# Rows of B and C written twice, one product in four moved to GpSimd, squares moved before a seam's decays: an audio tower with a selective scan on one core

## The chip, the cores and the metric

The kernel runs on one core of a Trainium2 chip. The metric is the device time of one execution in microseconds. The engines work in parallel, each through its own list of instructions in order, and wait for one another by semaphores: TensorE (PE, with its weight loads PEld), VectorE (DVE), ScalarE (ACT), GpSimd (POOL), and SyncE (SP), which here issues every DMA.

## The reference

Inputs are 64 series of 750 samples, cut into 10 overlapping patches of 128, so 640 tokens of width 512. The core of the reference, shortened:

```
h = patches @ W.T + b                                  # tokens, width 512
hid = layernorm(h);  x = rmsnorm(hid)
z, xv, B, C, dt_in = split(x @ in_proj_w.T)            # 1024, 256, 256, 1024, 128
dt = softplus(dt_in @ dt_proj_w.T + dt_proj_b)         # 1024 channels
state[ch, n] = exp(dt * A[ch, n]) * state[ch, n] + dt * xg[ch] * B[ch, n]   # 16 states, over 10 steps
y[ch] = sum_n C[ch, n] * state[ch, n] + D_skip * xg[ch]
mid = hid + (y * silu(z)) @ out_proj_w.T
h = h + mid + swiglu(rmsnorm(mid))                     # width 2048
h = h + swiglu(layernorm(h))                           # width 2048
```

## The kernel before

Tokens lie in the free dimension, channels on the 128 partitions. The tokens are worked in two chunks, of 290 and of 350 tokens (29 and 35 series of 10 steps). The scan is cut into **units**: for each of 8 tiles m of 128 channels, four units q of four states each, so 32 units a chunk, numbered u = 0 to 31 and 32 to 63. A partition of a unit holds one channel and four states; the width of a unit is 4 x 290 or 4 x 350 elements.

One unit goes through five engines. SP loads its rows of B into `bb` (L367) and of C into `cb` (L383), each row repeated over partitions. They come from `b_rows` and `c_rows` in DRAM, where SP has stored the projections five times over (L402 and L371), so that every unit's rows lie together. POOL multiplies dt * x (`dtx`, L443) by B into `hs` (L453), the input of the recurrence. ACT makes the decays exp(dt * A) in `da` (L551), a PSUM ring of ND = 4 pieces. DVE scans, four pieces a unit (L781), in place in `da`, and multiplies two pieces at a time by C into `hs` (L792). In chunk 0 PE adds the four states with an identity matrix into the bank `SUM` (L1000), unit u - 2 in the middle of slot u, and unit 31 at the end of slot 32. In chunk 1 POOL does these sums (`add_states`, L466 to L482). When a tile's four units are summed, DVE adds the skip and gates by z (L807, L813).

`hs` has NH = 4 slots. The input of unit u (L453) waits until the unit that held its slot has been summed: `h_summed` in chunk 0 (PE), `added` in chunk 1 (POOL).

All else is written into the **slots** of `schedule()`, one a unit, and every engine's program is made from that list, some kinds of step with a lag (`late`). In chunk 0's slots stand the projections of its later tiles (`in_c`, `in_z`, `dtp` for dt, `xs` for x), then, from unit 14 on, the norms of chunk 1 (`tokc`, `mean`, `ln1`, `rms1`), its projections and its first tiles. In chunk 1's slots stand chunk 0's output projection (`out`), and its two MLPs (`gu`, `down`), each led by a norm (`rms2`; `ln2_mean` and `ln2_var`). After unit 63 come chunk 1's own output and MLPs, which PE alone sets. A **seam** in this text is one of the two places where chunk 1's last projections (the steps in `SEAM`) stand beside a norm of chunk 0: there ACT makes four squares (L586), PE adds them over channels, ACT takes the inverse root (L592, L593), and DVE scales (L864, L880), before PE can start an MLP.

On ACT a slot is: decays of the unit's pieces 2 and 3, a first part of the steps, decays of pieces 0 and 1 of the next unit, the second part. POOL's slot is: the input of unit u + 1, the sums of unit u - 1, softplus of a tile (L488 to L492). SP's is: `load_b(u + 3)`, `load_c(u + 2)`. PSUM banks of the projections form a ring of three, later four. ACT loads a function table (L528) when it changes between ln/exp, silu and tanh.

## Time and profile before

| | us |
|---|---|
| median of 3 runs (lowest, highest) | 679.44 (677.98, 681.44) |
| the profiled execution, its own time | 676.66 |
| its span | 674.7 |
| PE busy in the span | 630.5 |
| DVE, POOL, ACT busy | 425.5, 428.9, 329.3 |

The profile is one execution, with the time of each instruction and, for each wait, the instruction that ended it. Some 2 us lie outside its span. The granted clock is TensorE's clock as a share of full speed, 1.00 being 2.4 GHz and 0.50 being 1.2 GHz. A float32 matmul is recorded as two instructions, so x8 is four matmuls.

### The profile page before, as it was taken

The numbers are of one execution on the slowest core, as the hardware profiler recorded it, in microseconds if no ns is written. First come the engines' busy times: TensorE is split into PE (matmuls) and PEld (weight loads), VectorE is DVE, ScalarE is ACT, GpSimd is POOL, SyncE is SP. The second block draws the span as 40 slices with busy tenths as digits, with TensorE's granted clock in tenths as the row PEclk, the third lists the DMA queues.
The fourth block names the chain that finished last, engine by engine and source line by source line (L and its number), as shares of the span: only waits on it lengthen the run. The fifth ranks groups of instructions, "written<-read, shape, count | busy, mean of one in ns | idle before, by whom it ended". The sixth has DMA issues, their size and how long they took to land.

```text
span 674.7 us, 8618 instructions
## 1 busy us (share of the span) xinstructions
PE 630.5 (93%) x2846; PEld 505.2 (75%) x2846; DVE 425.5 (63%) x660; ACT 329.3 (49%) x646; POOL 428.9 (64%) x244
## 2 busy tenths in 40 slices
PE   4959998799999979999979999999999999999998
PEld 3637675466665657777747777766999998999998
DVE  4087997889987859889887988861322223332132
ACT  4358888458887363323346323321642443543441
POOL 0276786348787999887877988644455464445561
PEclk9979999799999979999989999999999999999999
DMA  8799997599999949989866998634443353144421
GB/s 339 253 358 365 316 312 245 169 280 371 336 375 373 362 176 359 412 334 332 316 247 231 345 326 317 200 124 113 140 153 127 124 157 125 63 128 131 147 67 43
DMA packets 49164, 163.50 MB, mean 242 GB/s; under 512 B 4320, under 2 KB 18528, under 8 KB 48480
## 3 DMA queue, kind: packets, MB, share of 16 engines
q1 hardware_dynamic: 49120, 162.95, 69.6%
q8 instruction: 23, 0.38, 0.2%
q14 instruction: 21, 0.17, 0.1%
HBM read 145.24 MB, written 17.69 MB: 242 GB/s over the span
## 4 chain that ended last, share of the span: by engine, by line
PE 73%; DVE 12%; ACT 4%; POOL 4%; issue 3%; DMA 2%; SPq 0%; DVEq 0%; ACTq 0%; POOLq 0%
PE work L990 53%; PE da L990 15%; DVE da L781 7%; PE work L1000 5%; DVE hs L792 3%; POOL hs L453 2%; ACT L528 1%; DMA bb<-b_rows 1%; ACT da L551 1%; DMA c_rows<-c_rows 1%; DMA sm<-small 1%; POOL acc L479 0%; POOL acc L477 0%; POOL hs L466 0%; DVE a L847 0%
## 5 line engine op out<-in xcount | busy, mean ns | idle before, releaser
L781 DVE TENSOR_TENSOR_SCAN da<-da,hs 128x290 f32<-128x290 f32 (+1 forms) x256 | 198.1, 817 | 35.1 <-POOL hs L453 21.2
L453 POOL TENSOR_TENSOR hs<-dtx,bb 128x1160 f32<-128x1160 f32 (+1 forms) x64 | 171.1, 2674 | 59.6 <-PE work L1000 52.4
L551 ACT ACTIVATE da<-dt,a_neg 128x261 f32<-128x261 f32 (+1 forms) x256 | 118.4, 495 | 144.7 <-DVE hs L792 144.5
L432 POOL TENSOR_TENSOR ws<-wraw,ws 128x1024 fp32r<-128x1024 f32 x40 | 101.5, 2538 | 92.8 <-ACT ws L559 92.8
L990 PE MATMUL work<-sq,wraw 128*128 128x290 f32 x512 | 126.0, 407 | 1.5 <-DVE sq L880 1.1
L990 PE MATMUL work<-hn,win 128*128 128x290 f32 (+1 forms) x336 | 103.6, 457 | 17.4 <-DVE hn L855 8.0
L990 PEld LDWEIGHTS work<-sq,wraw 128*128 128x128 f32 x512 | 96.5, 189 | 30.8 <-issue 1.8
L792 DVE TENSOR_TENSOR hs<-da,cb 128x580 f32<-128x580 f32 (+1 forms) x128 | 105.3, 822 | 10.2 <-DMA cb<-c_rows 3.5
L990 PEld LDWEIGHTS work<-hn,win 128*128 128x128 f32 x336 | 65.7, 200 | 51.3 <-issue 26.1
L559 ACT CAST ws<-wraw 128x1024 fp32r<-128x1024 f32 x48 | 50.3, 1048 | 70.6 <-PE da L990 34.4
L990 PE MATMUL work<-hn,ws 128*128 128x350 f32 x480 | 79.2, 323 | 1.6 <-DVE hn L951 1.6
L990 PEld LDWEIGHTS work<-hn,ws 128*128 128x128 f32 x480 | 77.3, 189 | 1.9 <-issue 1.9
L1000 PE MATMUL work<-hs,sm 128*128 128x290 f32 x256 | 67.8, 408 | 0.0
L990 PE MATMUL work<-gated_n,wraw 128*128 128x290 f32 x256 | 63.3, 407 | 0.0
L1000 PEld LDWEIGHTS work<-hs,sm 128*128 128x128 f32 x256 | 48.5, 190 | 16.3 <-DVE hs L792 0.5
L990 PEld LDWEIGHTS work<-gated_n,wraw 128*128 128x128 f32 x256 | 48.5, 189 | 14.2
L990 PE MATMUL da<-hn,ws 128*128 128x350 f32 x288 | 47.5, 323 | 0.0
L990 PE MATMUL da<-gated,ws 128*128 128x350 f32 x288 | 47.0, 323 | 0.0
L990 PEld LDWEIGHTS da<-gated,ws 128*128 128x128 f32 x288 | 46.5, 189 | 0.0
L990 PEld LDWEIGHTS da<-hn,ws 128*128 128x128 f32 x288 | 46.4, 189 | 0.0
L899 DVE TENSOR_TENSOR pair<-th,work 128x350 f32<-128x350 f32 x20 | 10.4, 520 | 56.7 <-PE work L990 50.6
L477 POOL TENSOR_TENSOR acc<-acc,hs 128x700 f32<-128x700 f32 x16 | 26.7, 1666 | 19.6 <-DVE hs L792 19.6
(97 smaller groups left out, 630.8 us busy)
## 6 DMA issues: line engine op xcount, KB each, us to landing
wraw<-w_stream SPq DMA_DIRECT2D x104, 512.0 KB, 3.8
bb<-b_rows SPq DMA_DIRECT2D x32, 700.0 KB, 6.7
cb<-c_rows SPq DMA_DIRECT2D x32, 700.0 KB, 5.5
bb<-b_rows SPq DMA_DIRECT2D x32, 580.0 KB, 8.2
cb<-c_rows SPq DMA_DIRECT2D x32, 580.0 KB, 6.2
c_rows<-c_rows SPq DMA_DIRECT2D x8, 875.0 KB, 11.0
c_rows<-c_rows SPq DMA_DIRECT2D x8, 725.0 KB, 6.4
win<-w_in SPq DMA_DIRECT2D x4, 1024.0 KB, 13.1
```

Of the source, the lines that this page charges most:

```text
L432: nc.gpsimd.tensor_tensor(ws[:, k % NW, 1, :], wraw[:, split_loads[k] % NRAW, :], ws[:, k % NW, 0, :].bitcast(F32), ALU.subtract).then_inc ...
L453: nc.gpsimd.tensor_tensor(hs[:, u % NH, 0:NQ * n].rearrange("p (n t) -> p n t", t=n), dtx[:, t % 2, 0:n].unsqueeze(1).to_broadcast([P, NQ, ...
L477: nc.gpsimd.tensor_tensor(total, total, lo, ALU.add).then_inc(added, 1)
L528: nc.scalar.preload_act_table_set(name)
L551: last = nc.scalar.activation(dst, src, ACT.Exp, scale=a_neg[:, j:j + 1])
L559: nc.scalar.copy(ws[:, k % NW, 0, :], wraw[:, i % NRAW, :]).then_inc(w_hi_done, 1)
L781: nc.vector.tensor_tensor_scan(da[:, k % ND, 0:w], da[:, k % ND, 0:w], hs[:, u % NH, p * w:(p + 1) * w], 0.0, ALU.mult, ALU.add).then_inc( ...
L792: nc.vector.tensor_tensor(hs[:, u % NH, here].rearrange("p (i w) -> p i w", w=w), da[:, k % ND:k % ND + 2, 0:w], cb[:, u % NC, here].rearr ...
L899: nc.vector.tensor_tensor(gated_f[:, i % 2, 0:n], th[:, i % 2, 0:n], bank((s, "up")), ALU.mult).then_inc(gated_raw, 1)
L990: last = nc.tensor.matmul(dst, w, x, start=(k == 0), stop=(k == len(pairs) - 1))
L1000: last = nc.tensor.matmul(work[SUM][:, 0:n], sm[:, S_IDENT:S_IDENT + P], hs[:, u % NH, i * n:(i + 1) * n], start=(q == 0 and i == 0), stop ...
```

## The change

1. **Rows in DRAM.** `COPIES` goes from 5 to 2 for C, and B is stored 2 x 2 times (`COPIES`, `TWICE`), by four DMAs a half instead of one. The order of channels and states on the partitions is new, so that a load reads 16 rows of B for 8 partitions each (before 32 for 4) and 32 rows of C for 4 partitions each (before 128 for one). Bytes per load stay.
2. **Start.** The second half of B, `("in_b", 0, 1)`, moves from slot 0 to slot 1. The halves have semaphores of their own; tiles 0 to 3 wait for the first half alone.
3. **GpSimd multiplies.** In chunk 0, for units with u % 4 == 1 (8 of 32), DVE scans into `hs` instead of `da` and makes no product; POOL multiplies the unit by C in one instruction of 4 x 290 (`times_c` on POOL), behind the input of unit u + 2. The decays that reuse `da` wait for the scan there, the sums and the next load into the same `cb` for POOL's product.
4. **Slots.** Chunk 0 has five slots of 4 x 290 in `hs`, chunk 1 four of 4 x 350, which begin at the third. An input waits for the last unit that shares any of its columns. Units 32, 33 wait for the sums of 28 and 29 as before, unit 34 for 31 (before 30), unit 35 for 31.
5. **Seams.** The second part of ACT's steps is now halved at a seam also where it holds an `in_z` of `SEAM`, and after a silu in such a slot the table of exp and tanh is loaded, not that of ln and exp.

```diff
 NQ = 4
 QU = NS // NQ
 UNITS = KI * QU
+HS = 5 * NQ * TS[0]
 BANK = 512
...
 
-NH, NB, ND, NC = 4, 4, 4, 3
+NB, ND, NC = 4, 4, 3
+
+NH = (5, 4)
+FIRST_SLOT = (0, 2)
 
 NG = 3
...
 HH = HT // 2
 
 
-REPL = P // 8
-COPIES = (REPL + NQ - 1 + NQ - 1) // NQ
+
+COPIES, TWICE = 2, 2
 SPLITS = 4 * (HH + KD)
 LOADS = KD + SPLITS
...
     return u // UNITS, u % UNITS // QU, u % QU
+
+
+def slot_at(u):
+
+    c = u // UNITS
+    return (u % UNITS + FIRST_SLOT[c]) % NH[c] * NQ * TS[c]
+
+
+def slot_before(u):
+
+    def ends(v):
+        return slot_at(v) + NQ * TS[v // UNITS]
+    shared = [v for v in range(u) if slot_at(v) < ends(u) and slot_at(u) < ends(v)]
+    return max(shared, default=None)
 
 
...
+def on_pool(u):
+
+    return u < UNITS and u % QU == 1
+
+
 def products_through(u):
 
-    return piece(u, NP[u // UNITS] - 1) // 2 + 1
+    return 2 * len([v for v in range(u + 1) if not on_pool(v)])
+
+
+PRODUCTS = products_through(NCH * UNITS - 1)
 
 
 def recurrence(u):
 
+    if on_pool(u):
+        return [("scan", u, p) for p in range(4)]
     return [("scan", u, 0), ("scan", u, 1), ("times_c", u, 0), ("scan", u, 2), ("scan", u, 3), ("times_c", u, 1)]
 
...
@@ -110,9 +143,9 @@
 
 def schedule():
 
-    slots = [(None, [("bmean", 0), ("tokc", 0), ("mean", 0), ("ln1", 0), ("rms1", 0), ("in_dt", 0), ("in_b", 0, 0), ("in_b", 0, 1),
+    slots = [(None, [("bmean", 0), ("tokc", 0), ("mean", 0), ("ln1", 0), ("rms1", 0), ("in_dt", 0), ("in_b", 0, 0),
                      ("dtp", 0, 0), ("in_c", 0, 0), ("in_x", 0, 0), ("xs", 0, 0)]),
-             (None, [("in_c", 0, 1), ("in_x", 0, 1)])]
+             (None, [("in_c", 0, 1), ("in_b", 0, 1), ("in_x", 0, 1)])]
     bg = two_tiles(0, 1) + two_tiles(0, 3) + two_tiles(0, 5)
     bg[3].insert(0, ("in_z", 0, 0))
...
+            return hs[:, slot_at(u) + lo:slot_at(u) + hi]
+
+        def multiplied(eng, u):
+
+            if on_pool(u):
+                eng.wait_ge(c_times_pool, u // QU + 1)
+            else:
+                eng.wait_ge(c_times, products_through(u))
 
         def h(c, k):
...
-                rows = b_dram[c].rearrange("(o m n) t -> m o (n t)", m=KI, n=NQ)[m, 2 * q:2 * q + 2 * REPL]
-                src = rows.unsqueeze(1).to_broadcast([2 * REPL, 4, w])
+                if q == 0 and m % 4 == 0:
+                    b_in_dram(sp, c, m // 4)
+                rows = b_dram[c].rearrange("(o m n) t -> m o (n t)", m=KI, n=NQ)[m, 4 * q:4 * q + 16]
+                src = rows.unsqueeze(1).to_broadcast([16, P // 16, w])
                 sp.dma_start(bb[:, u % NB, 0:w], src).then_inc(bb_loaded[u % NB], 16)
 
...
-                    sp.wait_ge(c_times, products_through(u - NC))
+                    multiplied(sp, u - NC)
                 if q == 0:
                     sp.wait_ge(c_stored[m % 2], 16 * ((KI * c + m) // 2 + 1))
-                src = c_dram[c][m].rearrange("(o i n) t -> o i (n t)", i=4, n=NQ)[2 * q:2 * q + 2 * REPL]
+                rows = c_dram[c][m].rearrange("(o n) t -> o (n t)", n=NQ)[8 * q:8 * q + 32]
+                src = rows.unsqueeze(1).to_broadcast([32, P // 32, w])
                 sp.dma_start(cb[:, u % NC, 0:w], src).then_inc(c_loaded[u % NC], 16)
 
...
-                        sp.dma_start(b_dram[c].rearrange("(k i p) t -> i p k t", p=P, i=2)[i],
-                                     sq[:, 2 + i, 0:TS[c]].unsqueeze(1).to_broadcast([P, COPIES, TS[c]])).then_inc(
-                                         b_stored, 16)
+                        dst = b_dram[c].rearrange("(k y d i r) t -> k d i y r t", k=COPIES, d=TWICE, i=2, r=4 * NQ)
+                        for k in range(COPIES):
+                            for d in range(TWICE):
+                                sp.dma_start(dst[k, d, i], sq[:, 2 + i, 0:TS[c]]).then_inc(b_stored[i], 16)
                     if s[0] == "in_c":
                         store_c(*s[1:])
...
-                if u >= NH:
-                    v = u - NH
-                    if v < UNITS:
-                        pool.wait_ge(h_summed, v + 1)
-                    else:
-                        pool.wait_ge(added, adds_through(v + 1 if v % QU == 0 else v))
-                nc.gpsimd.tensor_tensor(hs[:, u % NH, 0:NQ * n].rearrange("p (n t) -> p n t", t=n),
+                v = slot_before(u)
+                if v is not None and v < UNITS:
+                    pool.wait_ge(h_summed, v + 1)
+                elif v is not None:
+                    pool.wait_ge(added, adds_through(v + 1 if v % QU == 0 else v))
+                nc.gpsimd.tensor_tensor(states(u, 0, NQ * n).rearrange("p (n t) -> p n t", t=n),
                                         dtx[:, t % 2, 0:n].unsqueeze(1).to_broadcast([P, NQ, n]),
                                         bb[:, u % NB, 0:NQ * n].rearrange("p (n t) -> p n t", t=n),
                                         ALU.mult).then_inc(dbx_done, 1)
+
+            def times_c(u):
+                c, w = u // UNITS, NQ * TS[u // UNITS]
+                pool.wait_ge(c_loaded[u % NC], 16 * (u // NC + 1))
+                pool.wait_ge(scan_done, piece(u, NQ - 1) + 1)
+                nc.gpsimd.tensor_tensor(states(u, 0, w), states(u, 0, w), cb[:, u % NC, 0:w], ALU.mult).then_inc(c_times_pool, 1)
 
             def add_states(u):
                 c, m, q = unit_of(u)
...
+                if unit is not None and unit >= 1 and on_pool(unit - 1):
+                    times_c(unit - 1)
                 if unit is not None and unit >= 1:
                     add_states(unit - 1)
...
                 act.wait_ge(dt_ready, c * KI + m + 1)
-                if k >= ND:
-                    act.wait_ge(c_times, (k - ND) // 2 + 1)
+
+                if k >= ND and on_pool(piece_of(k - ND)[0]):
+                    act.wait_ge(scan_done, k - ND + 1)
+                elif k >= ND:
+                    v, j = piece_of(k - ND)
+                    act.wait_ge(c_times, products_through(v) - 1 + j)
                 src = dt[:, m, 0:n].rearrange("p (b t) -> p b t", t=STEPS)[:, :, 1:]
                 for i in range(GS[c]):
...
-                    if not parts and not any(s[0] == "in_z" for s in second):
+                    if not parts and not any(s[0] == "in_z" and s not in SEAM for s in second):
                         n = len(second) // 2
                         first, second = second[:n], second[n:]
...
-                    log_tables()
+                    use_tables("exp_and_others" if any(s in SEAM for s in steps) else "natural_log_exp_and_others")
 
         @block.vector
...
                 dve.wait_ge(da_done, k + 1)
-                nc.vector.tensor_tensor_scan(da[:, k % ND, 0:w], da[:, k % ND, 0:w], hs[:, u % NH, p * w:(p + 1) * w], 0.0,
+                dst = states(u, p * w, (p + 1) * w) if on_pool(u) else da[:, k % ND, 0:w]
+                nc.vector.tensor_tensor_scan(dst, da[:, k % ND, 0:w], states(u, p * w, (p + 1) * w), 0.0,
                                              ALU.mult, ALU.add).then_inc(scan_done, 1)
 
```

What stands in a row on three places, before and after. In these rows `x8` is the number of instructions alike (matmuls once each).

PE from the norm of chunk 0 on; `hn` is the normed input, `win` the projections, `dti,wdt` the projection to dt, `sq,sm` that to x. Before:

```order
L990 MATMUL work<-hn,win 128x290 x12
L990 MATMUL work<-dti,wdt 128x290
L990 MATMUL work<-hn,win 128x290 x8
L990 MATMUL work<-sq,sm 128x290
L990 MATMUL work<-hn,win 128x290 x8
```

And after:

```order
L1054 MATMUL work<-hn,win 128x290 x8
L1054 MATMUL work<-dti,wdt 128x290
L1054 MATMUL work<-hn,win 128x290 x8
L1054 MATMUL work<-sq,sm 128x290
L1054 MATMUL work<-hn,win 128x290 x12
```

Four matmuls moved from ahead of the first dt to behind the first x. SP's queue at the same place, before:

```order
L402 DMA b_rows<-sq 128x5x290 [waits bank_free2]
L402 DMA b_rows<-sq 128x5x290 [waits bank_free0]
L371 DMA c_rows<-c_rows 128x5x290 [waits bank_free2]
L367 DMA bb<-b_rows 128x1x1160 [waits b_stored]
L383 DMA cb<-c_rows 128x1160 [waits c_stored0]
```

And after:

```order
L454 DMA b_rows<-sq 8x16x290 [waits bank_free2]
L454 DMA b_rows<-sq 8x16x290 x3
L419 DMA c_rows<-c_rows 128x2x290 [waits bank_free1]
L415 DMA bb<-b_rows 128x1x1160 [waits b_stored0]
L432 DMA cb<-c_rows 128x1x1160 [waits c_stored0]
```

Two stores of five copies have become four of one copy, and the second half's four stand behind the store of C's second tile. ACT at the first seam (`rms2`), before:

```order
L642 COPY c_rows<-work 128x350 [waits bank_full3,c_stored1]
L551 ACTIVATE da<-dt,a_neg 128x35x9 [waits c_times,dt_ready] x4
L586 ACTIVATE sq<-a 128x290 [waits res_done,b_stored,bank_full1]
L586 ACTIVATE sq<-a 128x290 [waits res_done] x3
L592 ACTIVATE rstd_ln<-work,cols 128x290 [waits bank_full0,norm_done]
```

And after:

```order
L705 COPY c_rows<-work 128x350 [waits bank_full3,c_stored1]
L612 ACTIVATE da<-dt,a_neg 128x35x9 [waits c_times,dt_ready] x2
L648 ACTIVATE sq<-a 128x290 [waits b_stored1,res_done,b_stored0,bank_full1]
L648 ACTIVATE sq<-a 128x290 [waits res_done] x3
L654 ACTIVATE rstd_ln<-work,cols 128x290 [waits bank_full0,norm_done]
L655 ACTIVATE work<-rstd_ln 128x290 [waits act_chain]
L612 ACTIVATE da<-dt,a_neg 128x35x9 [waits c_times,dt_ready] x2
```

Two decays moved from ahead of the squares to behind the inverse root. ACT at the second seam (`ln2_var`), before:

```order
L668 ACTIVATE z<-work 128x350
L528 ACT_TABLE_LOAD
L551 ACTIVATE da<-dt,a_neg 128x35x9 [waits c_times,dt_ready] x2
L586 ACTIVATE sq<-a 128x290 [waits centered2,bank_full0]
```

And after:

```order
L731 ACTIVATE z<-work 128x350
L585 ACT_TABLE_LOAD
L612 ACTIVATE da<-dt,a_neg 128x35x9 [waits c_times,dt_ready] x2
L585 ACT_TABLE_LOAD
L648 ACTIVATE sq<-a 128x290 [waits centered2,bank_full0]
```

The order of decays and squares is the same here, and a table load has been added between them.

## Rows read from the trace of the kernel before

**Rows 1.** Windows: stretch, length, busy PE PEld DVE ACT POOL, clock, DMA share, GB/s

```profile
66.00:107.00 41.00, 39.61 (x154) 27.87 (x152) 38.59 (x58) 32.56 (x74) 32.82 (x25) 1.00 0.94 318
126.00:191.00 65.00, 64.73 (x222) 42.72 (x223) 59.01 (x88) 45.22 (x100) 38.50 (x25) 0.96 0.94 314
240.20:341.00 100.80, 100.80 (x404) 77.33 (x405) 83.93 (x126) 38.40 (x79) 86.37 (x48) 0.98 0.88 324
```

**Rows 2.** Timeline of the start: start us, us, engine, line, instruction, [idle before <- releaser]

```profile
21.56 2.33 SPq L402 DMA_DIRECT2D b_rows<-sq  x2
...
26.50 0.36 SPq L371 DMA_DIRECT2D c_rows<-c_rows  x1
...
28.54 0.60 SPq L367 DMA_DIRECT2D bb<-b_rows  x1
...
30.76 0.34 SPq L383 DMA_DIRECT2D cb<-c_rows  x1
...
33.21 2.42 POOL L453 TENSOR_TENSOR hs<-dtx,bb 128x1160 f32<-128x1160 f32 x1 [3.14 <-DMA bb<-b_rows]
...
39.41 3.77 PE L990 MATMUL work<-hn,win 128*128 128x290 f32 x8 [6.13 <-ACT c_rows L642]
...
48.65 5.83 PE L990 MATMUL work<-hn,win 128*128 128x290 f32 x16 [1.47 <-ACT xf L652]
```

**Rows 3.** DMA issues to 60 us: count, KB each, median us from issue to landing

```profile
b_rows<-sq SPq DMA_DIRECT2D x2, 725.0 KB, 4.6
...
pat<-patches SPq DMA_DIRECT2D x1, 145.0 KB, 2.6
```

**Rows 4.** Windows, columns as in rows 1, of four us after the start

```profile
50.00:54.00 4.00, 4.00 (x12) 2.91 (x11) 3.86 (x7) 3.80 (x10) 1.98 (x1) 0.64 1.03 315
```

**Rows 5.** Timeline of units 10 to 14: PE's x step repeats each tile

```profile
83.84 0.75 PE L990 MATMUL work<-sq,sm 32*128 32x290 f32 x2
...
84.06 2.44 POOL L453 TENSOR_TENSOR hs<-dtx,bb 128x1160 f32<-128x1160 f32 x1 [1.74 <-PE work L1000]
...
89.76 2.45 POOL L453 TENSOR_TENSOR hs<-dtx,bb 128x1160 f32<-128x1160 f32 x1
...
98.72 2.19 PE L990 MATMUL work<-hn,win 128*128 128x290 f32 x8 [0.34 <-ACT z L668]
...
102.80 0.75 PE L990 MATMUL work<-sq,sm 32*128 32x290 f32 x2
...
106.28 0.88 ACT L551 ACTIVATE da<-dt,a_neg 128x261 f32<-128x261 f32 x2 [0.95 <-DVE hs L792]
```

**Rows 6.** Timeline of the change of chunks and the first seam

```profile
212.31 2.91 POOL L453 TENSOR_TENSOR hs<-dtx,bb 128x1400 f32<-128x1400 f32 x1 [2.96 <-PE work L1000]
...
212.87 2.22 PE L1000 MATMUL work<-hs,sm 128*128 128x290 f32 x8
...
229.62 1.67 DVE L781 TENSOR_TENSOR_SCAN da<-da,hs 128x350 f32<-128x350 f32 x2 [2.02 <-POOL hs L453]
...
235.96 0.97 ACT L551 ACTIVATE da<-dt,a_neg 128x315 f32<-128x315 f32 x2 [0.84 <-DVE hs L792]
...
239.52 1.43 ACT L586 ACTIVATE sq<-a 128x290 f32<-128x290 f32 x4
...
240.10 4.12 PE L990 MATMUL work<-sq,mean_w 128*128 128x290 f32 x8 [5.52 <-ACT sq L586]
```

**Rows 7.** Timeline of the second seam

```profile
348.07 0.97 ACT L551 ACTIVATE da<-dt,a_neg 128x315 f32<-128x315 f32 x2 [0.15 <-DVE hs L792]
348.99 1.43 ACT L586 ACTIVATE sq<-a 128x290 f32<-128x290 f32 x4
```

**Rows 8.** DMA issues of the whole run, columns as in rows 3

```profile
cb<-c_rows SPq DMA_DIRECT2D x32, 580.0 KB, 6.2
```

**Rows 9.** Groups by line and shape: count, busy us, mean ns, idle before and releasers

```profile
L792 DVE TENSOR_TENSOR hs<-da,cb 128x580 f32<-128x580 f32 x64 | 48.8, 762 | 4.4
...
L528 ACT ACT_TABLE_LOAD x25 | 32.1, 1283 | 5.1 <-PE work L990 4.0 <-PEq L1167 0.7
```

50 lines of the change are left out of this document (28 added, 22 removed).

## The prediction, made before the changed kernel was run

> **What bounds the kernel now.** I read the table of busy time by stretch first, then the chain of work that ended last, then the timeline where the two leave PE idle. PE is busy for 630.5 of 674.7 us, so an edit elsewhere pays only by what it takes out of PE's pauses and of its time at the low clock. The stretches say where those are. From 126 to 191 us, the second half of chunk 0, PE is busy for 64.7 of 65.0 us, and DVE for 59.0; from 240 to 341 us, the first MLP, PE has no pause at all [rows 1]. There a lighter DVE brings nothing. From 66 to 107 us PE (39.6) and DVE (38.6 of 41.0) are both full: the chain runs over DVE, but PE's x step comes at 83.84 and again at 102.80, 18.96 us for four units, and PE waits for 0.34 us of that [rows 5]. So PE would need 18.6 us a tile there, whatever DVE does. What is left are four places: the start, where PE waits 6.13 us for `c_rows` and 1.47 us for `xf` [rows 2]; the norm of chunk 1 near 107 to 126 us; and the two seams, with PE idle for 5.52 us at the first [rows 6] and waiting for the squares of 348.99 at the second [rows 7].
>
> **The start.** The projection of B's second half, 4 of the 12 matmuls ahead of the first dt, leaves PE's row; four take 2.19 us with their tail, the row of 98.72 [rows 5], so 2.0 us for all behind them. C's store goes from 26.50 to 24.5. The first half of B is in place at 21.56 as before and is now stored by four DMAs. Their landing is nowhere in the trace: a store of 725 KB takes 4.6 us, the load of 145 KB, one store's size, 2.6 us [rows 3]. Issued some 0.45 us apart, the last leaves at 23.0 and lands at 25.6 (by the large store's row 27.6). So `load_b(0)` goes from 28.54 to 25.6. C's store took 4.26 us (26.50 to the load that waited for it at 30.76); with 290 KB it lies between 2.6 and 4.26, I take 3, by the row of like size, and the load of C goes to 27.5, 3.3 us sooner. The input of unit 0 (33.21, [rows 2]) moves by 2.9 us, that of unit 1 by about 3, and with them DVE, the decays that ACT holds back, the copy of C behind these decays, and PE's restart at 39.41: **-2.9** (bounds -1 and -4).
>
> Then PE is behind the scan until DVE's first gate. Unit 1 has no product on DVE, 2 x 0.762 us less [rows 9], which lets ACT come to `xf` sooner; of the 1.47 us wait I take 0.9 away, since PE also has a dt product of half a microsecond to make in that stretch that it made in its pause before: **-0.9** (0 to -1.5). The eight matmuls that follow take 5.83 us, with the clock at 0.64 [rows 4], against 4.4 us for two groups of four at full clock [rows 5]. The fall came after PE's waits of 6.13 and 1.47 us. With the first cut to about 3.6 and the second nearly gone I take it that the clock stays up: **-1.4** (0 to -3.3, since the matmuls at 39.41 are slow as well). The fifth slot frees unit 5's input from PE's second sum, so that DVE isn't late here. The start is -5.2 together.
>
> The Trainium skill, TensorE: Matmul & The Clock Gate, section "The HAM clock gate", says that the throttled state is the default, and that the chip judges activity in windows that run free of the kernel. By that the clock term may or may not come, from one execution to the next; without it the forecast would be 1.4 us higher. No run here shows it yet.
>
> **GpSimd's products.** They take 1.52 us a tile off DVE, 8 times, 12.2 us. In the second half PE hides it: 0. In the first, PE's 0.34 us a tile are all there is, twice: **-0.7** (0 to -3). On POOL a product is new. The nearest row has the same width and two inputs from SBUF as well, 2.44 us [rows 5], and I take that. POOL is in order, so softplus and the input of the next tile's first unit are queued behind. Now POOL waits 1.74 us at 84.06 for PE's sum, and the next tile's input starts at 89.76, 1.4 us ahead of DVE's need [rows 5]. The fifth slot takes the wait away, the product takes 2.44: the input ends about 0.8 us later than a DVE relieved by 1.5 us wants it. DVE then needs 18.3 us a tile, still under PE's 18.6. The scan into SBUF and not PSUM I cost at nothing, between -0.1 and +0.1 us a scan. The load of C for every fourth unit waits for POOL's product, 3 to 4 us later than for DVE's; SP stands on it with the next load of B. A load of C takes 6.2 us by the median [rows 8], and two units of DVE, some 9 us, lie between the release and the use, so it is just in time.
>
> **The norm of chunk 1.** ACT waits 0.95 us for DVE's product of unit 13 [rows 5], which is one that leaves DVE, and PE waits on ACT there: **-0.9** (0 to -2). PE's other pause before 126 us hangs on a chain of ACT and DVE over units 15 and 16, which keep their products: 0.
>
> **Change of chunks and first seam.** The input of unit 34 (212.31) now waits for the sum of unit 31, not 30. PE ends that at 215.09 (212.87 and 2.22), 2.8 us later [rows 6]. POOL works without a pause from there on, and DVE waits for it for 2.02 us at 229.62, so I take the whole: **+2.8** at the decays of 235.96. Behind these the squares no longer wait for two more decays: they start at 236.93 plus the shift, not at 239.52: **-2.6**. Net +0.2 (bounds: +2.8 if the squares then wait for something else, -4.6 if POOL's delay is absorbed, the 2.6 plus some 2.0 because PE's eight records after the pause take 4.12 us, against 2.2 at full clock).
>
> **Second seam.** Decays and squares keep their order, 348.07 and 348.99, one right behind the other [rows 7], and a table load of 1.283 us [rows 9] now stands between, in PE's pause: **+1.3** (0.9 to 2). The load saved at the first seam comes where PE is full: 0. From there on PE sets the time and nothing is changed. Fewer stored bytes (C 725 to 290 KB a tile) relieve DMAs that hardly anyone waits for after the start: 0.
>
> **Sum.** -5.2 - 0.7 - 0.9 + 0.2 + 1.3 = -5.3 us. From the profiled execution's 676.66 us that is 671.4; the median of the three runs was 2.8 us above that execution, so for a median 679.44 - 5.3 = **674.1 us**.
>
> **Rivals.**
> - Only the first load comes sooner, the clock and the wait for `xf` stay: -2.9 - 0.7 - 0.9 + 0.2 + 1.3, and half of the small terms gone, about -2: 677.4, no change. For it: the slow clock has two causes, of which one stays. 0.26.
> - POOL's delay is absorbed and the seam shows its full gain: -5.2 - 0.7 - 0.9 - 4.6 + 1.3 = -10.1: 669.3. For it: POOL pauses 2.96 us before 212.31 [rows 6]. Against it: that pause is the same wait. 0.13. If DVE set the pace all through chunk 0, -12.2 would come on top of the start: 663. PE's full windows speak against it. 0.03.
> - **Slower**: POOL becomes the pace of chunk 0. If the rows of B come too late for the fifth slot to be used, the product stands fully in front of the next tile's input: 2.44 us, less a slack of 1.4, on a DVE that is 1.5 ahead, is 2.6 us of idle DVE a tile, 17.4 + 2.6 = 20.0 against 18.96 now; over three tiles +3.1. With the start at -2.9, the seam at +2.8 because the same POOL is late there, and +1.3: +4.3, 683.7. It decides when POOL's product ends over 1 us later than worked out. 0.09.
> - The four stores run one after the other: 4 x 2.6 us from 21.56 is 32.0, and the start is lost by 3.4 us where it gained 2.9: with the other terms +3.3, 682.7. Against it: the loads at 28 to 34 us are issued half a microsecond apart, and overlap. The Trainium skill (DMA: Bandwidth & Descriptors, section on the anatomy of one DMA) gives each DMA a fixed cost of about 2.0 us, mostly completion: by it four small ones in a row would be dearer than one. 0.04.
>
> **Chances.** 0.45 for the forecast. A measurement of this kernel tells about 0.5%, 3.4 us, from no change. Cases that end below 676.0 hold about 0.61, those within 676.0 to 682.8 about 0.28, above 0.11. The range for 8 in 10 goes from 666 (seam gain, or a full clock at the start) to 681.5.
>
> **What would show it.** In the trace after: DVE's first scan near 32.8 (before 33.21 + 2.42 = 35.6); PE's restart near 36.5 and the clock near 50 us at 1.0; still 18.6 us a tile from 66 us; POOL's product 2.44 us; input of unit 34 right behind the last sum of PE; squares of the first seam as long after that sum as before; a third table load before the second seam's squares and PE idle 1.3 us longer there. It would be wrong if a load of C is what DVE waits for at every fourth unit, if PE has pauses between 66 and 190 us, or if the start moves by less than a microsecond.

## The result, and the profile of the changed kernel

The changed kernel takes 719.05 us (median, 714.61 to 731.08), against 678.97 us for the kernel before on the same chip: 1.058 times as long, interval 1.055 to 1.061. The forecast was 674.1 us, with a range that ended at 681.5. It failed by 45 us and in its sign. Some executions of a kernel run a few per cent slower than its others at a lower granted clock: the times given for a kernel are medians of all its executions, ratios leave those out, and the profiles of `e_bb8s` and `e_cb8` are of such ones (750.8 and 752.4 us).

The profiled execution has a span of 716.7 us, 42.0 more than the 674.7 of before. From the page of the changed kernel: the engines' busy time, the shares by engine of the chain that ended last, and four rows of its DMA issues (how many, KB each, median us from issue to landing).

```profile
PE 641.3 (89%) x2846; PEld 507.3 (71%) x2846; DVE 413.9 (58%) x644; ACT 329.1 (46%) x646; POOL 449.7 (63%) x252
...
PE 48%; DMA 25%; DVE 12%; issue 5%; POOL 5%; ACT 4%; SPq 2%; DVEq 0%; ACTq 0%; POOLq 0%
...
wraw<-w_stream SPq DMA_DIRECT2D x104, 512.0 KB, 8.3
bb<-b_rows SPq DMA_DIRECT2D x32, 700.0 KB, 22.2
cb<-c_rows SPq DMA_DIRECT2D x32, 700.0 KB, 19.9
bb<-b_rows SPq DMA_DIRECT2D x32, 580.0 KB, 11.8
```

PE executes the same 2846 matmul instructions. It is idle for 75.4 us where it was for 44.2, which is 31.2 of the 42.0 us; the other 10.8 are a longer busy time for the same instructions, at a mean granted clock of 0.969 instead of 0.979. And DMAs, which held 2% of the chain before, hold a quarter of it. In the kernel before these four rows read:

```profile
wraw<-w_stream SPq DMA_DIRECT2D x104, 512.0 KB, 3.8
bb<-b_rows SPq DMA_DIRECT2D x32, 700.0 KB, 6.7
cb<-c_rows SPq DMA_DIRECT2D x32, 700.0 KB, 5.5
...
bb<-b_rows SPq DMA_DIRECT2D x32, 580.0 KB, 8.2
```

A load of B of chunk 1 (700 KB) takes over three times as long to land, and so does one of C; one of weights, on the same queue, takes twice as long, and a load of B of chunk 0 (580 KB) 11.8 us instead of 8.2. The table of waits says who stands for it (us in total, times, longest):

```profile
ACT da L612 <- DVE hs L856: 168.4, 83, 9.8
POOL hs L502 <- DMA bb<-b_rows: 101.1, 35, 9.6
...
DVE hs L856 <- DMA cb<-c_rows: 33.7, 19, 11.3
...
PEld work L1054 <- DMA wraw<-w_stream: 24.7, 13, 2.9
```

GpSimd waits 101.1 us for rows of B (before 6.0). The stretch from 260 to 330 us, first in the kernel before and then in the changed one, shows how the DMA engines work: packets and rate, then the queue's packets, MB and busy share of 16 engines.

```profile
DMA packets 5857, 24.69 MB, mean 353 GB/s; under 512 B 640, under 2 KB 855, under 8 KB 5851
...
q1 hardware_dynamic: 5851, 24.62, 94.5%
```

```profile
DMA packets 4640, 19.03 MB, mean 272 GB/s; under 512 B 504, under 2 KB 760, under 8 KB 4635
...
q1 hardware_dynamic: 4635, 18.97, 99.5%
```

The engines are busier and move less. One packet holds its engine for 0.945 x 16 x 70 us / 5851 = 0.181 us before and for 0.995 x 16 x 70 / 4635 = 0.240 us after, on average. Split by size in the traces of the same stretch, it is mainly the packets of 5600 bytes that grow, one for each partition of a load of B or C in chunk 1: from 237 to 367 ns on average. The packets of 4096 bytes, of weights, go from 177 to 199 ns. Over the whole run 91% of the 5600-byte packets took less than 240 ns before, and 14% after. Half of them belong to C, whose load has 32 blocks: what B's load does to its own packets it does to C's as well. The first two stretches of [rows 1], the first MLP where it now lies, and two more, in the changed kernel (us, busy time and count of PE, PEld, DVE, ACT, POOL, clock, DMA share, GB/s):

```profile
66.00:107.00 41.00, 40.25 (x157) 28.80 (x158) 33.16 (x50) 33.12 (x75) 36.71 (x25) 1.00 0.95 261
...
126.00:191.00 65.00, 60.52 (x207) 39.63 (x206) 53.08 (x81) 39.81 (x91) 42.28 (x26) 0.95 0.82 234
...
261.60:370.20 108.60, 98.85 (x385) 74.07 (x384) 82.73 (x123) 35.21 (x73) 78.76 (x44) 0.97 1.01 267
...
341.00:385.00 44.00, 32.84 (x108) 23.16 (x107) 28.01 (x40) 14.43 (x26) 27.81 (x16) 0.85 1.02 260
385.00:484.00 99.00, 88.62 (x354) 65.87 (x353) 75.99 (x115) 34.84 (x74) 71.18 (x39) 1.00 1.00 265
```

PE was without a pause in the first MLP [rows 1]; now it is idle for 9.8 us of it and, from 385 to 484 us, for 10.4 us of the second, with the DMA engines at 1.01 and 1.00. The loss can be dated by DVE's gate of the first tiles and by PE's mean of squares at the seams, in the changed kernel:

```profile
73.34 0.46 DVE L877 TENSOR_TENSOR yg<-work,z 128x290 f32<-128x290 f32 x1
92.29 0.46 DVE L877 TENSOR_TENSOR yg<-work,z 128x290 f32<-128x290 f32 x1
...
257.27 2.19 PE L1054 MATMUL work<-sq,mean_w 128*128 128x290 f32 x8 [1.93 <-ACT sq L648]
...
380.91 4.21 PE L1054 MATMUL work<-sq,mean_w 128*128 128x290 f32 x8 [6.23 <-ACT sq L648]
```

Before, the same rows began at 65.63, 84.58, 240.10 [rows 6] and 349.56 us. So 7.7 us are lost up to the first gate, none from there to the second gate, 9.5 more up to the first seam, 14.2 up to the second and 10.6 behind it.

The start itself, which was to gain 5.2 us (SPq rows are DMAs that SP issues):

```profile
22.64 2.63 SPq L454 DMA_DIRECT2D b_rows<-sq  x4
...
25.62 0.39 SPq L419 DMA_DIRECT2D c_rows<-c_rows  x1
...
29.12 0.61 SPq L415 DMA_DIRECT2D bb<-b_rows  x1
...
34.76 2.42 POOL L502 TENSOR_TENSOR hs<-dtx,bb 128x1160 f32<-128x1160 f32 x1 [5.56 <-DMA bb<-b_rows]
37.22 1.42 DVE L845 TENSOR_TENSOR_SCAN da<-da,hs 128x290 f32<-128x290 f32 x2 [19.75 <-POOL hs L502]
```

### The profile page after: what moved, and what is told of

Read it like the earlier page. It is cut to its first block, busy times and chain, and to the rows that moved or that the text cites. A ratio compares the mean times of both kernels' runs of the same rounds, so it can differ in the third digit from the quotient of the medians.

```text
span 716.7 us, 8626 instructions
## 1 busy us (share of the span) xinstructions
PE 641.3 (89%) x2846; PEld 507.3 (71%) x2846; DVE 413.9 (58%) x644; ACT 329.1 (46%) x646; POOL 449.7 (63%) x252
## 2 busy tenths in 40 slices
DMA packets 42572, 154.98 MB, mean 216 GB/s; under 512 B 4384, under 2 KB 11936, under 8 KB 41888
## 4 chain that ended last, share of the span: by engine, by line
PE 48%; DMA 25%; DVE 12%; issue 5%; POOL 5%; ACT 4%; SPq 2%; DVEq 0%; ACTq 0%; POOLq 0%
PE work L1054 32%; PE da L1054 14%; DMA wraw<-w_stream 13%; DMA cb<-c_rows 7%; DVE da L845 6%; DMA bb<-b_rows 4%; DVE hs L856 3%; POOL hs L502 2%; PE work L1064 2%; POOL hs L511 1%; ACT L585 1%; SPq L454 1%; ACT da L612 1%; DMA b_rows<-sq 1%; DMA sm<-small 1%
## 5 line engine op out<-in xcount | busy, mean ns | idle before, releaser
L502 POOL TENSOR_TENSOR hs<-dtx,bb 128x1160 f32<-128x1160 f32 (+1 forms) x64 | 171.0, 2675 | 109.0 <-DMA bb<-b_rows 101.1
L845 DVE TENSOR_TENSOR_SCAN da<-da,hs 128x350 f32<-128x350 f32 (+1 forms) x224 | 175.5, 826 | 37.7 <-POOL hs L502 24.4
L1054 PE MATMUL work<-sq,wraw 128*128 128x290 f32 x512 | 129.8, 412 | 15.3 <-DMA wraw<-w_stream 14.2
L1054 PE MATMUL work<-hn,win 128*128 128x290 f32 (+1 forms) x336 | 107.4, 469 | 16.2 <-DVE hn L919 8.0
L856 DVE TENSOR_TENSOR hs<-da,cb 128x700 f32<-128x700 f32 (+1 forms) x112 | 93.1, 831 | 38.2 <-DMA cb<-c_rows 33.7
L1054 PE MATMUL work<-gated_n,wraw 128*128 128x290 f32 x256 | 66.0, 416 | 4.8 <-DMA wraw<-w_stream 4.8
L963 DVE TENSOR_TENSOR pair<-th,work 128x350 f32<-128x350 f32 x20 | 10.4, 520 | 56.8 <-PE work L1054 50.7
## 6 DMA issues: line engine op xcount, KB each, us to landing
bb<-b_rows SPq DMA_DIRECT2D x32, 700.0 KB, 22.2
bb<-b_rows SPq DMA_DIRECT2D x32, 580.0 KB, 11.8
```

Source lines behind the costliest of these rows:

```text
L502: nc.gpsimd.tensor_tensor(states(u, 0, NQ * n).rearrange("p (n t) -> p n t", t=n), dtx[:, t % 2, 0:n].unsqueeze(1).to_broadcast([P, NQ, n] ...
L845: nc.vector.tensor_tensor_scan(dst, da[:, k % ND, 0:w], states(u, p * w, (p + 1) * w), 0.0, ALU.mult, ALU.add).then_inc(scan_done, 1)
L856: nc.vector.tensor_tensor(states(u, lo, hi).rearrange("p (i w) -> p i w", w=w), da[:, k % ND:k % ND + 2, 0:w], cb[:, u % NC, lo:hi].rearra ...
L963: nc.vector.tensor_tensor(gated_f[:, i % 2, 0:n], th[:, i % 2, 0:n], bank((s, "up")), ALU.mult).then_inc(gated_raw, 1)
L1054: last = nc.tensor.matmul(dst, w, x, start=(k == 0), stop=(k == len(pairs) - 1))
```

## The experiments

Two theories stood after that. **A**: the load of B is slow by itself, by the way its rows are now read. **B**: GpSimd, with its products and the fifth slot, holds buffers back so that loads are issued late. The table gives all runs; a ratio is to the kernel before on the same chip, and the last column is the median landing of a 700 KB load of B (empty for `e_bb8i` and `e_bb4i`, where the profile gives none, and for the small parts, where it is 6.5 to 6.9 us). C's own 700 KB load lands in 22.2 us in `e_cb8` and in 20.6 in `e_c16d`.

| run | what differs from the kernel before | us | ratio, interval | B lands |
|---|---|---|---|---|
| after | the whole change | 719.05 | 1.058, 1.055 to 1.061 | 22.2 |
| e_rest | the change without the rows and the start | 679.98 | 1.0025, 1.0007 to 1.0043 | 6.8 |
| e_rows | the new rows alone | 717.32 | 1.056, 1.052 to 1.060 | 21.0 |
| e_bb8 | load of B: 16 rows x 8 partitions | 736.72 | 1.084, 1.080 to 1.089 | 22.1 |
| e_cb4 | load of C: 32 groups x 4 | 679.46 | 1.0011, 0.9994 to 1.0029 | 6.6 |
| e_bb8s | B: 16 x 8, neighbours on other rows | 740.80 | 1.091, 1.086 to 1.095 | 24.2 |
| e_bb8d | B: 16 x 8, rows twice as far apart | 737.14 | 1.089, 1.085 to 1.094 | 23.0 |
| e_cb8 | C: 16 x 8 | 740.79 | 1.083, 1.079 to 1.087 | 23.2 |
| e_bb8i | B: 8 blocks of 16 rows | 835.33 | 1.221, 1.215 to 1.226 | |
| e_bb4i | B: 4 blocks of 32 rows | 987.68 | 1.458, 1.454 to 1.461 | |
| e_c16d | C: 16 x 8, nothing shared | 741.21 | 1.091, 1.083 to 1.100 | 22.8 |
| e_b4p | B: 32 x 4, four rows in all | 677.62 | 0.9991, 0.9975 to 1.0006 | 6.4 |
| e_fix | the change, B stored four times, 32 x 4 | 694.29 | 1.026, 1.023 to 1.028 | 6.1 |
| e_seam | squares ahead of decays alone | 674.03 | 0.9947, 0.9930 to 0.9963 | |
| e_seam2 | the same again | 674.53 | 0.9949, 0.9932 to 0.9965 | |
| e_seamt | seam and choice of table | 676.52 | 0.9977, 0.9961 to 0.9993 | |
| e_slot5 | seam and five slots | 677.51 | 0.9996, 0.9980 to 1.0013 | |
| e_prod7 | seam, five slots, seven products | 678.52 | 1.0002, 0.9989 to 1.0015 | |
| e_best | seam and start | 676.02 | 0.9970, 0.9949 to 0.9991 | |

### Rows or products

`e_rest` is the changed kernel with the old rows, stores and loads, and B's second half back in the first slot of the schedule. `e_rows` is the kernel before with the new rows, stores and loads. `e_bb8` and `e_cb4` change one load each of the kernel before:

```diff
-rows = b_dram[c].rearrange("(o m n) t -> m o (n t)", m=KI, n=NQ)[m, 2 * q:2 * q + 2 * REPL]
-src = rows.unsqueeze(1).to_broadcast([2 * REPL, 4, w])
+rows = b_dram[c].rearrange("(o m n) t -> m o (n t)", m=KI, n=NQ)[m, 2 * q:2 * q + 16]
+src = rows.unsqueeze(1).to_broadcast([16, P // 16, w])
```

```diff
-src = c_dram[c][m].rearrange("(o i n) t -> o i (n t)", i=4, n=NQ)[2 * q:2 * q + 2 * REPL]
+rows = c_dram[c][m].rearrange("(o n) t -> o (n t)", n=NQ)[8 * q:8 * q + 32]
+src = rows.unsqueeze(1).to_broadcast([32, P // 32, w])
```

> The changed kernel with the old rows in DRAM: five copies of B and C, the old channels on the partitions, the old loads and stores, B's second half back in slot 0. GpSimd's products, the five slots and the seams stay. Theory A (the loads from the new rows are slow, nothing else is): the time falls back to near the kernel before, 676 to 681 us, and the DMAs move some 350 GB/s again from 260 to 330 us, where the changed kernel moves 272. Theory B (GpSimd's products or the slots hold back the releases of the buffers, and the DMAs only look slow because loads stand on each other): it stays above 705 us.

> The kernel before with the new rows in DRAM alone: two copies of C, two times two of B, the new channels, loads of B from 16 rows for 8 partitions each, of C from 32 rows for 4 each. No product on GpSimd, four slots, old seams. Theory A: all of the loss is here, 710 to 722 us, with 260 to 275 GB/s in the window 260 to 330 us. Theory B: 672 to 680 us, since fewer bytes are stored.

> The kernel before, where only the load of B reads the first 16 of its 32 rows, each for 8 partitions instead of 4; the numbers in B's partitions 64 to 127 are others than the reference's. Bytes, copies and stores stay. Theory A with 8 readers of a row as the cause: most of the loss, 700 to 715 us, and B's load of 700 KB takes over 12 us to land (6.2 before). Theory A with C's loads as the cause: 678 to 682.

> The kernel before, where only the load of C reads 32 groups of four rows for 4 partitions each, instead of 128 groups for one each; the states are multiplied by other rows of C than the reference's. Bytes, copies and stores stay. Theory A with 8 readers of B as the cause: at most a small part, 679 to 690 us. Theory A with C's loads as the cause: 700 to 715, and C's load of 700 KB takes over 12 us to land (5.5 before).

Theory B falls: without the new rows the change costs 0.25%, 1.7 us. The rows alone cost 5.6%, 38 us; the two add up to the 40 measured, although `e_rest` leaves out the start too. And B's load needs no other edit to do it: alone it costs 8.4%, more than the 700 to 715 us expected, while C's costs nothing that can be measured. `e_rows` also has the new stores of B, by fours; their part in its 38 us is looked at with `e_fix` below. That `e_bb8` is 19 us slower than `e_rows` fits its stores: it moves 163.50 MB in all and `e_rows` 154.98, and where the DMA engines are full at some 280 GB/s, 8.5 MB are 30 us of their time by this estimate.

### What about the load is slow

I took it to be the eight readers of one row, and tried first whether it matters that they are neighbours (`e_bb8i`), that they read the same addresses (`e_bb8s`), how far apart the rows are (`e_bb8d`), and whether B is special (`e_cb8`).

```diff
# e_bb8i
+src = rows.unsqueeze(0).to_broadcast([P // 16, 16, w])
# e_bb8s
+src = bass.AP(tensor=rows.tensor, offset=rows.offset, ap=[[step, 16], [step, 8], [1, w]])
# e_bb8d: every second of 32 rows
+src = rows.unsqueeze(1).to_broadcast([16, P // 16, w])
# e_cb8: the first 16 of C's groups
+src = rows.unsqueeze(1).to_broadcast([16, P // 16, w])
```

> The kernel before, with the load of B reading 16 rows eight times over, as in the slow one with eight readers, but the readers of one row are 16 partitions apart (partition p reads row p mod 16), so that the partitions that one after another fetch are all on different rows. B's values reach the wrong partitions; the amount and the shape of the work are unchanged. With neighbours as readers it took 736.7 us, a load of B landed after 22.1 us, and 276 GB/s were moved between 260 and 330 us. Theory 'neighbours': what hurts is that neighbouring partitions fetch the same row; then this is back near 679 to 685 us, B lands in 6 to 8 us, 340 to 355 GB/s. Rival 'few rows': what hurts is that a load touches only 16 rows of 4.6 to 5.5 KB; then this stays at 725 to 740 us, with B's landing near 20 us.

> The kernel before, with the load of B reading 16 starting rows, and of each starting row eight neighbouring partitions, where each partition starts one small row (a quarter of what it fetches) further than its neighbour. It fetches as many bytes, from nearly as small a piece of memory as with eight readers a row, but neighbours no longer fetch the same addresses at the same moment. B's values are not the right ones; the work is unchanged. Theory 'same address at the same moment': 679 to 690 us, B lands in 6 to 8 us, 340 to 355 GB/s between 260 and 330 us. Rival 'small footprint': near 735 us, B's landing near 21 us, 270 to 280 GB/s.

> The kernel before, with the load of B reading every second one of its 32 rows for eight neighbouring partitions, so that the 16 pieces lie 74 KB apart (90 in chunk 1) instead of 37. B's values are not the right ones; the work is unchanged. Theory 'few pieces' (16 pieces are too few, wherever they lie): as with eight readers at 37 KB, 730 to 740 us, a landing near 20 us. Rival 'spacing': engines that stand at 74 KB from each other, as they do with four readers, are free, so 679 to 684 us, a landing of 6 to 8 us.

> The kernel before, with the load of C reading 16 groups for eight neighbouring partitions each, where each group is one piece of 4.6 or 5.5 KB right behind the last one (B's rows of the same size are 37 KB apart in chunk 0). C's values reach the wrong partitions; the work is unchanged. With 32 groups and four readers it took 679.5 us, the same as before. Theory 'few pieces': any load that reads only 16 pieces is slow, so this is 720 to 740 us and C lands after some 20 us. Rival 'B's spacing': only rows that are 37 KB apart (44.8 in chunk 1) get in each other's way, so this stays at 678 to 682 us and C lands in 5 to 7 us.

In `e_bb8s` the step is the distance of two rows of `b_dram`, not the quarter of a fetch that the expectation says: neighbours there read whole different rows, 23 in all. It was as slow as with eight neighbours on one row. So were the rows twice as far apart, and C's contiguous groups. All this spoke for "16 pieces are too few", and `e_bb8i`, at 835 us outside what either theory gave, for an extra loss when readers are spread. `e_bb4i` was to part the number of pieces from their readers; it has 32 pieces, as the fast load has:

```diff
-src = rows.unsqueeze(1).to_broadcast([2 * REPL, 4, w])
+src = rows.unsqueeze(0).to_broadcast([4, 2 * REPL, w])
```

> The kernel before, with the load of B reading its 32 rows four times over, the readers of one row 32 partitions apart (partition p reads row p mod 32) instead of neighbours. B's values reach the wrong partitions; the work is unchanged. With 16 rows the same spread took 835 us against 737 for neighbours. Theory 'number of pieces': 32 pieces are enough, however their readers lie: 678 to 682 us, B lands in 6 to 8 us. Rival 'same piece at the same time': four readers that belong to four different DMA engines meet on one row, which neighbours, served one after another by one engine, do not: 710 to 760 us, B's landing over 15 us.

At 988 us it is the slowest of all, outside what either theory gave. Its page shows DMA engines that are idle while everybody waits for them (queue row, and the chain's shares):

```profile
q1 hardware_dynamic: 48352, 162.95, 54.6%
...
DMA 64%; PE 25%; DVE 5%; SPq 2%; POOL 2%; ACT 1%; issue 1%; POOLq 0%; ACTq 0%; DVEq 0%
```

54.6% busy, with DMAs on 64% of the chain. The order of the slow ones is that of the outermost number in the load's description: 4 blocks 988 us, 8 blocks 835, 16 blocks 737 to 741, 32 blocks 678. That made a third theory, that the shape decides and readers don't. The last two runs part these: `e_c16d` has 16 blocks of 8 with nothing shared, `e_b4p` 32 blocks of 4 that all read the same four rows.

```diff
# e_c16d
+src = bass.AP(tensor=rows.tensor, offset=rows.offset, ap=[[9 * step, 16], [step, 8], [1, w]])
# e_b4p
+rows = b_dram[c].rearrange("(o m n) t -> m o (n t)", m=KI, n=NQ)[m, 2 * q:2 * q + 4]
+src = rows.unsqueeze(0).to_broadcast([2 * REPL, 4, w])
```

> The kernel before, with the load of C written as 16 blocks of 8 pieces, all 128 pieces distinct: nobody reads what another partition reads (blocks lie 9 pieces apart, the pieces of a block next to each other). C's values are not the right ones; the work is unchanged. Theory 'shape': what is slow is a load described as 16 blocks of 8, because the DMA engines then share the work in another way, and the number of readers has nothing to do with it; the four spread readers (4 blocks of 32: 988 us) and the eight spread ones (8 blocks of 16: 835 us) stand in the order of their number of blocks. Then this is 730 to 745 us, C lands after 20 us or more, and a packet of 5.6 KB takes 350 ns or more on average instead of 237. Rival 'readers': without shared pieces this is as before, 677 to 681 us, C lands in 5 to 7 us.

> The kernel before, with the load of B written as 32 blocks of 4 as before, but every block reads the same four rows: 4 pieces for 32 readers each. B's values are not the right ones; the work is unchanged. Theory 'shape': 32 blocks of 4 are fast whatever they read: 677 to 684 us, B lands in 6 to 8 us. Rival 'few pieces' or 'same piece at the same time': this is the hardest case of either, above 740 us.

From 260 to 330 us, `e_c16d` and then `e_b4p`:

```profile
DMA packets 4759, 18.64 MB, mean 266 GB/s; under 512 B 467, under 2 KB 1170, under 8 KB 4754
...
bb<-b_rows SPq DMA_DIRECT2D x8, 700.0 KB, 18.5
```

```profile
DMA packets 5995, 24.87 MB, mean 355 GB/s; under 512 B 639, under 2 KB 1000, under 8 KB 5989
...
bb<-b_rows SPq DMA_DIRECT2D x9, 700.0 KB, 6.1
```

This settles it. A load of 128 distinct pieces is slow when it is written as 16 blocks of 8, and one with 32 readers a piece is as fast as before when it is written as 32 blocks of 4. In `e_c16d` the 5600-byte packets take 352 ns on average, in `e_b4p` 234. The greater part of the changed kernel's loss is the shape of its load of B. The readers that I had blamed from the start do nothing.

Why the shape matters, no run here shows directly. The Trainium skill has what fits it. DMA: Bandwidth & Descriptors, section "Why a DMA increments its semaphore by 16 and not by 1", says that a DMA runs on the largest number of engines, up to 16, that divides the outermost dimension of both sides: 4 and 8 engines for the 4 and 8 blocks. The 54.6% above agree, and so does the order of 988 and 835. By the same rule 16 and 32 blocks both use all 16 engines, so it doesn't tell these two apart. The same page's section "The descriptor swizzle", with SBUF — State Buffer, "Door 1: The DMA port swizzle", says that in an ordinary 128-partition transfer one engine writes two groups of four partitions, 32 apart, which belong to one port of SBUF, and that eight neighbouring partitions belong to two ports. With blocks of 8 each engine may thus write to two ports and meet another there. Packets of 367 instead of 237 ns, in C's load as well, are what one would see; that the engines are dealt out so in either shape is argued, not shown.

### The change with a fast load

`e_fix` stores B's rows four times and not twice, so that the load can be 32 x 4 again, and keeps all else of the change.

```diff
-COPIES, TWICE = 2, 2
+COPIES, TWICE = 2, 4
-rows = ...[m, 4 * q:4 * q + 16]
-src = rows.unsqueeze(1).to_broadcast([16, P // 16, w])
+rows = ...[m, 8 * q:8 * q + 32]
+src = rows.unsqueeze(1).to_broadcast([32, P // 32, w])
```

> The changed kernel with B's rows stored four times and not twice, so that a load of B reads 32 rows for 4 partitions each, as the kernel before does; C keeps 32 rows for 4 partitions, and everything else of the change stays: the second half of B projected later, GpSimd's products, five slots, squares ahead of decays. If the eight readers of a row are the whole loss, this is the change without it: 674 to 681 us (the prediction's parts give 674; the parts without the start measured 680.0, which with my start term of up to -5.2 is 675 to 680), B lands in 6 to 8 us, and 340 us of GB/s or more between 260 and 330 us. If the ordering of B's two halves or the separate stores also hurt, it is above 682. At the start eight stores instead of four stand ahead of the first load of B: I expect that load to start at 29 to 31 us and the start to gain nothing.

The loads land in 6.1 us, and the ratio falls from 1.058 to 1.026, some 22 of the 40 us. It is still above the 682 us beyond which something else had to hurt. SP's timeline shows what may:

```profile
143.89 7.87 SPq L454 DMA_DIRECT2D b_rows<-sq  x8
151.81 0.97 SPq L415 DMA_DIRECT2D bb<-b_rows  x1
...
153.78 5.98 SPq L454 DMA_DIRECT2D b_rows<-sq  x8
...
126.00:191.00 65.00, 56.07 (x187) 36.72 (x186) 48.64 (x75) 36.44 (x82) 40.64 (x25) 0.92 0.73 250
```

Eight stores take SP 7.9 and 6.0 us to issue, where one store with its copies inside took about half a microsecond, and the loads of B and C stand behind them. The new stores also have another shape, 8 blocks of 16 rows and not 128 rows with five copies; which of the two costs the time was not tested. PE does 56.07 us of work in a stretch where `e_rest` does 63.96. It hits the start too: POOL waits 12.1 us for rows of B between 39 and 66 us. The first load of B is issued at 32.71, later than the 29 to 31 expected. The changed kernel has stores in fours, 2.63 us a group at the start and 3.0 and 3.2 us near 150 us.

No run has the new stores alone. `e_fix` is some 15 us above `e_rest`, and of what else differs between them C's load costs nothing (`e_cb4`) and the start at most 2 us (`e_best`, below), so the stores are left for the most of it, by elimination. How much of the loss is theirs in the changed kernel can be bounded by dates. The mean of squares at the first seam begins at 254.07 in `e_fix`, 14.0 us later than before, and of its 15.5 us in all only 1.5 are lost behind it. The changed kernel loses 17.2 us up to that seam and 24.8 behind it, where no row of B is stored any more (the last store is issued at 154.3). So by these dates some 23 of the 42 us are the slow load's; how the 17.2 in front are shared between the load and the stores isn't separated.

### The small parts

`e_seam` changes one condition of ACT's order in the kernel before, `e_seamt` adds the change's table line:

```diff
-if not parts and not any(s[0] == "in_z" for s in second):
+if not parts and not any(s[0] == "in_z" and s not in SEAM for s in second):
# e_seamt besides
-log_tables()
+use_tables("exp_and_others" if any(s in SEAM for s in steps) else "natural_log_exp_and_others")
```

> The kernel before with one edit of the change alone: at the first seam the squares stand ahead of the next unit's decays; the table choice is left as it was, so no table load is added at the second seam. By the prediction's working, without GpSimd's products (whose five slots made the +2.8 us) this saves the 2.6 us of the squares, and up to 2.0 us more by PE's clock: 674.5 to 677 us, PE's pause ahead of the first MLP (5.5 us) shrinks to about 3 or less. Rival: the decays that now come later delay DVE's last unit by as much: 679 us, no change.

> The seam edit (674.0 us) together with the change's new choice of ACT's table, which puts a load of 1.28 us between decays and squares of the second seam. By the prediction's term of +1.3 us: 675.3 us, and PE's pause ahead of the second MLP 1.3 us longer. Rival: the load is hidden, or another one that goes away elsewhere pays for it: 674.0. With this run what GpSimd's products and the fifth slot cost is the difference to 680.0 us, which the kernel with all but the rows measured: +4.7 us if the table costs 1.3.

The seam alone makes the kernel 0.53% faster, and 0.51% when run again, a little more than expected. ACT and PE at the first seam in `e_seam`, to be held against [rows 6]:

```profile
236.59 0.97 ACT L551 ACTIVATE da<-dt,a_neg 128x315 f32<-128x315 f32 x2 [0.73 <-DVE hs L792]
237.50 1.43 ACT L586 ACTIVATE sq<-a 128x290 f32<-128x290 f32 x4
...
238.08 3.64 PE L990 MATMUL work<-sq,mean_w 128*128 128x290 f32 x8 [2.76 <-ACT sq L586]
```

The squares follow the first pair of decays without the second, and PE's pause is 2.76 us and not 5.52 (3.16 in `e_seam2`). At the second seam `e_seamt` has a table load between decays and squares, and PE's pause is 6.25 where `e_seam` has 4.85:

```profile
347.15 1.28 ACT L528 ACT_TABLE_LOAD   x1
348.44 1.45 ACT L586 ACTIVATE sq<-a 128x290 f32<-128x290 f32 x4
...
349.03 4.21 PE L990 MATMUL work<-sq,mean_w 128*128 128x290 f32 x8 [6.25 <-ACT sq L586]
```

The time, 676.5 us, is 1.2 above the 675.3 expected.

Then slots and products, each on top of the seam edit; in `e_slot5` the test for GpSimd's units returns False, in `e_prod7` it leaves out the last tile of chunk 0.

> The kernel before with the seam edit alone, once more, as the base of the next two on the same chip. It measured 674.0 us, 0.9947 of before [0.993, 0.9963]; I expect 0.993 to 0.997.

> The seam edit and the change's five slots for states in chunk 0, without any product on GpSimd: every unit's product stays on DVE, rows and table as before. All of the change but rows and table measured 1.0025 of before, and with seam edit and table alone 0.9977, so products and slots together cost 0.5%, 3.3 us. Theory 'slots': the cost is the input of unit 34, which with five slots of chunk 0 and four of chunk 1 waits for the sum of unit 31 instead of 30: then this is 676.5 to 677.5 us, and that input waits near 213 to 216 us. Rival 'products': it stays at 674 us.

> As the one with five slots, but with GpSimd's products too, in all tiles of chunk 0 but the last, where unit 29's product stays on DVE. In the trace with all eight products the last one stands at 194.07 us, ahead of softplus and of the input of unit 32, which comes 1.2 us later than before. Theory 'last product': without it the change of chunks is as in the run with slots alone, or better by what DVE was spared: at most that time. Rival 'every product': DVE's seven saved products bring nothing where PE is full, and the load of C that waits for GpSimd costs at the start: 1 to 2 us above the run with slots alone.

The fifth slot costs 0.9996 - 0.9949 = 0.5%, 3.2 us. Two rows of `e_slot5`:

```profile
214.58 2.90 POOL L497 TENSOR_TENSOR hs<-dtx,bb 128x1400 f32<-128x1400 f32 x1 [5.90 <-PE work L1057]
...
217.52 1.67 DVE L838 TENSOR_TENSOR_SCAN da<-da,hs 128x350 f32<-128x350 f32 x2 [1.96 <-POOL hs L497]
```

The input of unit 34 waits 5.90 us for PE's sum, against 2.95 in `e_seam2` and 2.96 before [rows 6], and DVE waits for it. GpSimd's products are worth nothing: `e_prod7` is 0.0006 above `e_slot5`, inside both intervals. Seven fewer products on DVE changed nothing in the first tiles; DVE's gates in `e_prod7` come at 65.88, 84.83 and 103.78 us, 18.95 apart, as they do before (65.63, 84.58, 103.53) and in the changed kernel.

`e_best` has the seam edit and the start: B's second half is projected later and the halves have semaphores and planes of their own in DRAM, so that each is one store with five copies inside and every load stays 32 x 4.

```diff
-sp.dma_start(b_dram[c].rearrange("(k i p) t -> i p k t", p=P, i=2)[i],
+sp.dma_start(b_dram[c][i].rearrange("(k p) t -> p k t", p=P),
-rows = b_dram[c].rearrange("(o m n) t -> m o (n t)", m=KI, n=NQ)[m, 2 * q:2 * q + 2 * REPL]
+rows = b_dram[c][m // 4].rearrange("(o m n) t -> m o (n t)", m=4, n=NQ)[m % 4, 2 * q:2 * q + 2 * REPL]
```

> The kernel before with the seam edit and the change's start alone: B's second half is projected behind the second projection of C, its store has a semaphore of its own, and the rows of the two halves lie in two planes of B's DRAM tensor, each stored five times by one DMA as before; every load reads 32 rows for 4 partitions, 18.6 KB apart in chunk 0. No products on GpSimd, four slots, old choice of table. The prediction's start was -5.2 us with bounds of -1 and -8.8; without GpSimd's part in it (the unit without product, 0.9) I now expect the first load of B at 26.5 to 28 us instead of 28.5, and 671 to 673.5 us in all. Rival: PE only pauses longer ahead of the x projection and the second half's four matmuls come due in a full stretch: 674 to 675.

It is faster than before by 0.3%, and not faster than the seam alone: its ratio is 0.2% higher, with intervals that overlap. At 676.0 us it misses both what I expected (671 to 673.5) and the rival (674 to 675). PE in `e_best`:

```profile
37.87 1.06 PE L996 MATMUL work<-dti,wdt 128*128 128x290 f32 x2 [3.75 <-ACT c_rows L648]
...
47.19 4.49 PE L996 MATMUL work<-hn,win 128*128 128x290 f32 x16 [0.95 <-ACT xf L658]
...
55.32 2.19 PE L996 MATMUL work<-hn,win 128*128 128x290 f32 x8 [1.68 <-ACT xf L658]
59.80 0.73 PE L996 MATMUL work<-dti,wdt 128*128 128x290 f32 x2 [2.29 <-ACT z L674]
```

The first load of B is issued at 27.04 and not 28.76 as in `e_seam`, and PE restarts at 37.87 and not 39.78. That is with a dt product which stood ahead of the pause; the four matmuls behind it start at 38.72, 1.1 us sooner. The eight matmuls near 48 us take 4.49 us and not 5.83, at a better clock. Then it all goes: PE waits 0.95, 1.68 and 2.29 us, 4.9 together, where `e_seam` waits 1.64 and 0.23; DVE waits 2.99 us for a load of C at 51.87, and the first gate comes at 67.06, where `e_seam` has 66.45 and its repetition `e_seam2` 67.14: nothing is left that can be told from the spread of one kernel.

## Why the prediction was wrong

**The step that failed** is a sentence behind the second seam: "Fewer stored bytes (C 725 to 290 KB a tile) relieve DMAs that hardly anyone waits for after the start: 0". It counted the stores and left the loads of these rows as they were, at 6.2 us for C by [rows 8]; B's landed in 6.7 and 8.2 us. But the change had rewritten the load itself, from 32 blocks of 4 partitions to 16 blocks of 8, 64 times in the kernel and on a queue whose engines were busy for 94.5% of the first MLP already. No term and no rival had a price for that. B's load of 700 KB went from 6.7 to 22.2 us, and the rows, loads and stores together, are 38 of the 40 us (`e_rows`). The load's shape has at least some 23 of them, by the dates of `e_fix`, and is enough to cost 57 us where the stores stay as they were (`e_bb8`). The second thing priced at nothing was the stores' hold on SP in the middle of the kernel: "fewer stored bytes" came as four DMAs for one, 3.0 and 3.2 us a group. A load whose description changes needed a look at the engines, even when its bytes don't.

**The start, -5.2.** In the changed kernel it came out at the other sign: POOL's first input at 34.76 against 33.21. Four small stores, the first at 22.64 and not 21.56, issued in 2.63 us, were not in place before 29.12, 3.9 us after the last was issued; I had said 25.6, with 2.6 us for it. The rival "four stores one after the other" isn't what happened: in `e_fix` four stores more take 3.1 us more to issue and put the first load off by 3.6, not by 4 x 2.6. The fixed cost of 2.0 us that this rival took from the Trainium skill (DMA: Bandwidth & Descriptors, "Anatomy of one DMA — SWDGE (gpsimd) path") is given there for DMAs that GpSimd issues, and here SP issues them. And the load took 5.6 us where it took 4.7. With stores and loads put right (`e_best`) the first-load term came in part, 1.9 us at PE's restart against 2.9, or 1.1 by the same matmuls, and the clock came back, the 1.4. By the Trainium skill (TensorE: Matmul & The Clock Gate, "The HAM clock gate") activity is judged in windows that run free of the kernel, so it might or might not; in this profile it did, 0.95 from 39 to 66 us against 0.86. None of it reached the end. My error there was to take the restart for the end of the start: PE's waits behind it grew by 3 us and took all back by the first gate.

**GpSimd's products, -0.7 and -0.9.** Measured 0. The main argument, that PE and not DVE sets the tile, held, to the point that not even the 0.34 us came. At the norm of chunk 1 the -0.9 hung on ACT's wait for DVE, which I had put down to the product that moves. With it moved, ACT still waits 0.95 us there and PE 1.26, as before (`e_prod7`, `e_rest`), so that wait isn't for this product. On POOL a product takes 2.65 us, not 2.44.

**Change of chunks and first seam, +2.8 and -2.6.** Both mechanisms were right. The fifth slot costs 3.2 us. The squares' move brings 3.6 us by its ratio: PE's pause is 2.8 us shorter, and its eight records take 3.64 and not 4.12 us, which I had left in the bounds. Together they are -0.4 where I said +0.2.

**Second seam, +1.3.** The pause grows by 1.4 us, as forecast, and the run by 2.0 (0.9977 - 0.9947), with intervals that touch. PE is at a lower clock around the longer pause, 0.92 against 0.96 from 341 to 385 us, which may be the rest.

These small parts sum to +1.7 us (`e_rest`), where the prediction's terms for them gave -0.1. What is still open is the port by port reason of the slow shape, what the new stores cost by themselves, and who keeps the tile at 18.95 us to the hundredth in kernels with 12 us less work on DVE.

**What would show it.** Of the signs that were named, two came: PE pauses for 4.5 us between 126 and 191 us, and the start didn't move by a microsecond in the wanted direction, but by 1.5 in the other. DVE's wait for C came too, but in 19 units and for another reason.

## What to carry to other kernels

When a change rewrites the access pattern of a DMA that runs often, price the load itself and not its bytes alone: hold its blocks against those of a load whose landing the trace shows, and time the new shape once on its own before anything is built on it. Many small stores in place of one with copies inside hold the queue's engine for their issue (6.0 and 7.9 us for eight, 0.43 for one), and what stands behind is late. A gain at a restart counts only at the next point where the engines meet.

The version worth keeping is the kernel before with one condition changed, 674.0 and 674.5 us.

## What the runs showed of the hardware

- A load of 128 partitions with 5600 bytes each lands in 4 to 7 us by the median when written as 32 blocks of 4 partitions and nothing slow is beside it, and in 21 to 24 as 16 blocks of 8, at any source: 128 distinct pieces, 16 rows or 23. With 4640 bytes each it is 8.2 us before and 11.8 to 15.4 in the runs with B as 16 blocks. It slows all that shares the queue: weights 3.8 to 8.3 us, and 353 to 272 GB/s in all.
- The loss shows in the packets: one of 5600 bytes takes 237 ns on average in the kernel before and 367 in the changed one (260 to 330 us), also in C's load with its 32 blocks, and one of 4096 bytes 177 and 199.
- How many partitions read one piece of DRAM doesn't matter, up to 32 readers of each (`e_b4p`, 0.9991).
- With 8 and 4 blocks outermost the kernel takes 835 and 988 us, the latter with DMA engines 54.6% busy.
- Eight stores of 175 KB, each written as 8 blocks of 16 rows, took 6.0 and 7.9 us to issue on SP, 0.75 to 1 us each; one store of 875 KB with five copies inside took 0.43.
